# Where the attention's log-count tiles are masked, and where the out-degrees are summed

## The reference, cut to what matters

```python
aw = einsum(q[src], k[dest]); m = segment_max(aw, src); e = exp(aw - m[src])      # 8 heads, 20000 edges
alpha = e / segment_sum(e, src)[src];  out = segment_sum(alpha * v[dest], src)
deg_out = clip(segment_sum(ones, src), 1)      # third layer; deg_in likewise from dst
```

## Time and profile before

| | |
|---|---|
| median of 3 runs | 852.57 us (851.87 to 854.69) |
| profiled execution | 853.61 us, span of its instructions 851.6 us |
| PE busy | 803.9 us (94%) |
| DVE busy | 571.5 us (67%) |
| ACT busy | 395.4 us (46%) |
| mean granted TensorE clock | 0.983 |
| DMA | 126.65 MB |

### The profile page before, as it was taken

One profiled execution on the slowest core, in us unless ns is written; L12 is line 12 of the kernel. 1 busy time (PEld: TensorE's weight loads), 2 busy tenths in 40 slices (PEclk: granted clock), 3 DMA queues, 4 the chain that ended last, 5 costly groups with the idle time before them and its releaser, 6 DMA issues.

```text
span 851.6 us, 16427 instructions
## 1 busy us (share of the span) xinstructions
PE 803.9 (94%) x5245; PEld 550.0 (65%) x5245; DVE 571.5 (67%) x1869; ACT 395.4 (46%) x710; POOL 213.1 (25%) x382
## 2 busy tenths in 40 slices
PE   5998998999999999999999989999987999987996
PEld 2456555447777777877778766777755445666673
DVE  6479989546777988888778446555557835975121
ACT  1334444546667667676666533333331223533331
POOL 4200000000021122022022332222228822574443
PEclk9999999999999999999999989999999999997998
DMA  9909977688100443332483636555515470085550
GB/s 251 347 19 226 230 215 212 144 285 239 34 27 30 124 134 97 107 84 62 158 299 107 201 109 178 175 163 167 165 53 146 114 222 25 25 277 129 186 167 19
DMA packets 89029, 126.65 MB, mean 149 GB/s; under 512 B 41071, under 2 KB 50447, under 8 KB 88686
## 3 DMA queue, kind: packets, MB, share of 16 engines
q1 hardware_dynamic: 75342, 107.45, 42.5%
q0 software_dynamic: 13600, 18.11, 7.5%
HBM read 64.89 MB, written 63.33 MB: 151 GB/s over the span
## 4 chain that ended last, share of the span: by engine, by line
PE 75%; DVE 12%; DMA 4%; POOL 3%; issue 3%; ACT 1%; SPq 1%; DVEq 0%; POOLq 0%; ACTq 0%
PE ps L805 18%; PE ps L687 11%; PE ps L698 10%; PE ps L716 10%; PE ps L936 6%; PE ps L614 5%; DVE R_B L1922 4%; PE ps L812 4%; PE ps L619 4%; DVE R_B L1921 2%; PE ps L967 2%; DMA R_A<-slots_d 1%; PE ps L758 1%; DMA slots_d<-R_B,slot 1%; PE ps L555 1%
## 5 line engine op out<-in xcount | busy, mean ns | idle before, releaser
L805 PE MATMUL ps<-R_B,R_A 128*128 x612 | 184.1, 443 | 1.7 <-ACT R_A L1476 0.6
L805 PEld LDWEIGHTS ps<-R_B,R_A 128*128 128x128 f32 x612 | 110.9, 192 | 34.3 <-issue 24.5
L1281 ACT ACTIVATE R_A<-R_A,neg_max 125x1250 f32<-125x1250 f32 x80 | 106.4, 1330 | 19.1 <-DVE neg_max L1966 19.1
L1966 DVE CUSTOM_DVE_ANT_0 R_A<-ps,R_B,neg_max 125x417 f32<-125x417 f32 (+1 forms) x160 | 96.2, 648 | 21.2 <-PE ps L687 21.2
L698 PEld LDWEIGHTS ps<-ident,R_A 125*125 125x125 f32 x800 | 93.7, 188 | 14.8 <-issue 13.2
L698 PE MATMUL ps<-ident,R_A 125*125 125x125 f32 x800 | 102.0, 277 | 0.7 <-ACT XN L1224 0.7
L687 PE MATMUL ps<-R_B 64*125 64x417 f32 (+1 forms) x480 | 101.7, 536 | 0.2
L716 PE MATMUL ps<-R_W,XN 125*64 125x125 f32 x1600 | 94.7, 272 | 1.1
L716 PEld LDWEIGHTS ps<-R_W,XN 125*64 125x64 f32 x1600 | 85.5, 136 | 15.5 <-issue 14.2
L1288 ACT ACTIVATE R_W<-ps 125x500 f32<-125x500 f32 x120 | 66.1, 586 | 48.7 <-PE ps L698 48.7
L614 PE MATMUL ps<-XT,R_W 128*128 128x500 f32 (+1 forms) x192 | 72.4, 522 | 0.7 <-ACT XT L1207 0.7
(11 more groups left out here) (280 smaller groups left out, 1169.4 us busy)
## 6 DMA issues: line engine op xcount, KB each, us to landing
slots_d<-R_B SPq DMA_DIRECT2D x9, 2322.0 KB, 10.7
R_B<-in_L_ffn_w_dram SPq DMA_DIRECT2D x28, 512.0 KB, 8.2
R_A<-slots_d SPq DMA_DIRECT2D x27, 256.0 KB
slots_d<-R_A SPq DMA_DIRECT2D x27, 256.0 KB
counts_d<-R_A SPq DMA_DIRECT2D x10, 546.9 KB
logs_d<-R_B SPq DMA_DIRECT2D x10, 546.9 KB
R_B<-counts_d SPq DMA_DIRECT2D x10, 546.9 KB
R_B<-logs_d SPq DMA_DIRECT2D x9, 546.9 KB
```

The costliest lines, as they stand in the source:

```text
L805: ins = pe.matmul(bank(b, TM, width), lhs[:, c * TM:c * TM + TM], flat[:, bass.ds(e * (n * width) + c * width, width)], start=c == 0, stop ...
L1281: act.activation(SC[u % 2][h], SC[u % 2][h], ACT.Exp, bias=neg_max[:, 2 * (u % 2) + h:2 * (u % 2) + h + 1], scale=-1.0, accum_out=den[:, 2 ...
L1966: dve.tensor_tensor_reduce(SC[u % 2][h][:, a:z], bank(2 * h + g % 2, P, z - a), logs[:, a:z], -1.0, least if t else 3.0e38, ALU.add, ALU.m ...
```

## The change

`mask_logs` keeps only its first operation, for the source tile 0; what it left in `logs_d` for the other nine tiles is now unmasked, and the store waits for ACT's logarithm and no longer for DVE. The nine tiles are masked after they are loaded, in LNB, by one operation over 1250 columns for each (`mask_tile(i)`), at the end of unit 4(i-1)+1: u = 1, 5, 9, ..., 33 for i = 1 to 9. The wait for the load moves with it. ACT waits, before it overwrites a log stage, for the small mask of block b-2. SyncE waits for all ten small masks before its first load of count rows. The out-degrees are summed at the ends of units 12, 15, 16, 19, 20, 23, 24, 27, 28 and 31 in place of 12, 14, ..., 30. SyncE's list keeps its order.

```diff
-OUT_DEGREE_AT = 12
+OUT_DEGREE_OF = {u: n for n, u in enumerate((12, 15, 16, 19, 20, 23, 24, 27, 28, 31))}
@@ SyncE
-                sp.wait_ge(S("ln_masked"), b + 1)
+                sp.wait_ge(S("ln_made"), b + 1)
                 move(logs_d[:, b * P:b * P + P].rearrange("(i p) d -> p i d", p=P), ln_stage[b % 2], logs_out[b % 2])
...
+            sp.wait_ge(S("ln_masked"), T)
             load_counts_of(range(5))
@@ ACT, counts_and_logs
                 above_zero(act, logs_out[k], (b - k) * 16)
+                above_zero(act, S("ln_masked"), b - 1)
@@ DVE
             def mask_logs(b, k):
                 dve.wait_ge(S("ln_made"), b + 1)
-                first, rest = ln_stage[k][:, 0, :], ln_stage[k][:, 1:T, :]
+                first = ln_stage[k][:, 0, :]
                 own = LN0[:, b * P:b * P + P] if isinstance(b, int) else LN0[:, bass.ds(b * P, P)]
-                dve.scalar_tensor_tensor(own, first, FAR, first, ALU.mult, ALU.min)
-                dve.scalar_tensor_tensor(rest, rest, FAR, rest, ALU.mult, ALU.min).then_inc(S("ln_masked"), 1)
+                dve.scalar_tensor_tensor(own, first, FAR, first, ALU.mult, ALU.min).then_inc(S("ln_masked"), 1)
...
                     if t == 0:
-                        if u == 0:
-                            dve.wait_ge(S("ln_masked"), T)
-                        elif j == 0:
-                            dve.wait_ge(logs_in[i % 2], 32 * (i // 2) + 32 * (i % 2))
+                        if j == 0:
+                            dve.wait_ge(S("ln_masked"), T + i)
...
+                def mask_tile(i):
+
+                    dve.wait_ge(logs_in[i % 2], 32 * (i // 2) + 32 * (i % 2))
+                    dve.scalar_tensor_tensor(LNB[i % 2], LNB[i % 2], FAR, LNB[i % 2], ALU.mult, ALU.min)\
+                       .then_inc(S("ln_masked"), 1)
...
-                    if u >= OUT_DEGREE_AT and u % 2 == 0 and u < OUT_DEGREE_AT + 2 * T:
-                        out_degree((u - OUT_DEGREE_AT) // 2)
+                    if u % PAIRS == 1 and u // PAIRS + 1 < T:
+                        mask_tile(u // PAIRS + 1)
+                    if u in OUT_DEGREE_OF:
+                        out_degree(OUT_DEGREE_OF[u])
```

## The result

| | before | after |
|---|---|---|
| median | 853.57 us (851.87 to 854.69, 4 runs) | **881.11 us** (878.15 to 886.23, 4 runs) |
| ratio | | **1.0322** (95%: 1.029 to 1.0354) |
| profiled execution | 853.61, span 851.6 | 886.23, span 884.4 |
| mean granted clock | 0.983 | 0.971 |

The changed kernel is slower by 27.5 us; forecast were 20, with a range of 862 to 880, just missed. The direction, the places and the mechanism were those of the forecast; several sizes were not.

What follows compares the result with a forecast made beforehand. Counting was taken as bound mostly by DVE, the attention by TensorE. The terms -8.5 + 3.3 + 4.4 + 3.7 + 10.8 + 6.3 gave +20.0 us, on the median of 852.6 a forecast of 872.6 us, range 862 to 880.

Steps and rivals of the forecast that it cites:

- stop of tile 9: Attention: the moved last out-degree sum delays the load to 447.5, so the score operation is 11.0 late: +10.8 us.
- counting: Counting stage: large masks removed from DVE; block-by-block sum 7.0, up to 9.9 with DVE running ahead; taken as -8.5 us.
- behind the attention: The rest of the kernel after the attention only shifts, its loads waiting for TensorE's and DVE's own progress: no loss.
- out-degree sums, in themselves: Attention: the moved sums fit DVE's idle time at the ends of units with u % 4 = 3: cost 0.
- five early masks: Attention units 5, 9, 13, 17, 21, logs already landed: TensorE loses 0.65 us at each, +3.3 us.
- stop of tile 7: Attention: logs' last traffic at 379.95, mask until 381.4, score operation 4.6 late, less 0.15 slack: +4.4 us.
- stop of tile 8: Attention: logs' last traffic at 409.8, mask ends at 411.2, score operation 3.8 late: +3.7 us.
- clock behind the three: TensorE after the three long stops: granted clock drops each time, losing 1.7, 1.7 and 2.9: +6.3 us.
- The load overtaking: Attention: tile 9's load gets in place at 440.4, its stop shrinks to 3.7: 865.5 us, chance 0.10.
- the stops without a clock drop: Attention: stops cost no clock drop, or DVE takes part of them back: +13.7, 866 us, chance 0.16.
- The fourth rival: Waits longer than they look, counting squeezing the transfers, or counting winning only 6 us: 878 us and more, chance 0.12.
- The faster outcome: Attention: the late loads come in time and counting wins: -3.3, 849 us, chance 0.04.

Runs made afterwards that it cites:

- e5: The kernel before with only the out-degree sums moved to units 12, 15, 16, ..., 31, masks in counting as before: 864.33 us, ratio 1.0117.
- e8: The changed kernel with an empty operation in place of the mask of nine tiles, behind the same wait: 870.92 us, ratio 1.0177.
- second look: The changed kernel run once more, unaltered, for a second profile: 879.07 us, ratio 1.0283 to the kernel before.
- e6: The changed kernel with the out-degree sums back in units 12, 14, ..., 30, all else as changed: 873.03 us, ratio 1.0202.
- e4: The changed kernel with each mask one unit later, right before the score operation that needs it: 866.56 us, ratio 1.0133.
- The first experiment: The changed kernel with only SyncE's list reordered, every load of logs issued as soon as its buffer is free: 852.76 us, ratio 0.9986.
- e2: The changed kernel with only tile 9's load of logs put ahead of its store and the expert loads: 863.96 us, ratio 1.0108.

## Why the prediction was right, and where it was not

The median of 881.11 us lies above the range of 862 to 880. The mechanism held, and four terms of the sum had the wrong size. First, the late loads were taken to be usable at their last traffic, and the waits ended 0.5 to 0.6 us behind it: 1.7 us over the three stops. Second, in "the load at 422.5 + 25.0 = 447.5" the last traffic came 26.8 us behind the store, not 25.0; with the first this makes the stop of tile 9 13.3 us where 10.8 were forecast. Third, counting gave 6.95 us, not 8.5. Fourth, "The rest of the kernel, behind the attention, only shifts" put at 0 what was 6.9 and 3.8 us in two profiles, and its cause is open. The ends of its own terms reached from 856 to 881; the median fell into the corner that it left out.

| step | forecast us | measured us | |
|---|---|---|---|
| counting | -8.5 | -6.95 | 1.5 too much |
| out-degree sums, in themselves | 0 | 0 beside the masks | 0.7 and 1.0 in e5 and e8 |
| five early masks | +3.3 | +3.3 | right |
| stop of tile 7 | +4.4 | +4.85 | 0.45 short |
| stop of tile 8 | +3.7 | +4.5 | 0.8 short |
| stop of tile 9 | +10.8 | +13.3 | 2.5 short |
| clock behind the three | +6.3 | +6.8 | sum right, parts not |
| end of the attention | +20.0 | +25.9 | |
| behind the attention | 0 | +6.9, second look +3.8 | open |

- **Counting.** The block-by-block sum, 7.0, was the measurement. What failed was "The eight slots let DVE run ahead while TensorE is the limit, and it spends that lead in block 7": block 7 takes 127.67 - 117.72 = 9.95 us and no less. By the starts of the blocks 1.24 us are saved in block 2 and in block 3, 0.83 in block 4, 0.52 in 5 and 6 together, 1.26 and 1.25 in 7 and 8, and 0.6 from block 9 on. The clock of 68 to 72 us stayed at 1.00 where it had been 0.57; that bought nothing to see, as block 3 is DVE's. The window after:
```profile
68.00:72.00 4.00, 3.79 (x24) 2.61 (x23) 4.00 (x19) 2.84 (x6) 0.00 (x0) 1.00 1.16 166
```
  The run without masks, at 6.5 us, is in line with it.
- **Early masks.** The starts of L749 stand 31.25 us apart between tiles at 251.84 and 283.09, where 30.56 stood (440.84 - 410.28). All five together give 3.3. The clock did not fall behind stops of 0.35 to 0.7 us (granted 1.00 from 215 to 360 us). The sums, in the same tiles, add nothing there: with the sums back (e6) these tiles are as long.
- **Tiles 7 and 8.** The stops ran 0.5 and 0.8 over. The last traffic came where it was forecast (379.95 and 409.8, moved by the -3.65 and +3.85 us won and lost up to then, give 376.3 and 413.65; it ended at 376.2 and 413.9). But the masks start 0.5 and 0.6 us behind it, where the forecast let them start at once; that makes 4.9 and 4.3. The run with the wait alone shows them 1.4 to 1.6 shorter, which is the mask's own 1.37: wait plus mask.
- **Tile 9** carried the largest error. The step was "25.0 us behind the end of the last out-degree sum", a distance copied from another moment. The time of that sum came out: 422.5, moved by -6.95 and by the 3.3, 4.85, 2.65, 4.5 and 2.6 us lost up to then, gives 433.45, and the store that follows it is issued at 433.47. But the mask started only at 460.91. Of the 2.5 us missing, 0.6 are again the time from the last traffic to the end of the wait. The rest, 1.8, is the transfers: their last traffic was at 441.1 before, 25.0 us behind the issue of the store, and now at 460.3, 26.8 us behind it. It was 25.2 with the sums back (425.91 to 451.1) and 26.2 in the second look (432.35 to 458.6). The list is the same in all, and in these four so are the bytes. The traffic before (416 to 441.2 us), after (433.4 to 461), and with only the sums moved (423.3 to 452.5):

```profile
DMA packets 4517, 7.57 MB, mean 300 GB/s; under 512 B 551, under 2 KB 2087, under 8 KB 4515
...
DMA packets 4517, 7.55 MB, mean 274 GB/s; under 512 B 552, under 2 KB 2088, under 8 KB 4516
...
DMA packets 5366, 8.41 MB, mean 288 GB/s; under 512 B 582, under 2 KB 2935, under 8 KB 5363
```
  So the changed kernel moved no more, only more slowly. With only the sums moved it is another case, 29.1 us to the end of the wait (423.34 to 452.46): three expert loads that stand behind the logs in SyncE's list were issued from 443.25 on, before the logs were there, and 0.8 MB more was moved. The run with the mask before its use (e4) has the same, 8.31 MB and 28.9 us. SyncE's list, after:

```profile
433.47 0.75 SPq L338 DMA_DIRECT2D planes_d<-R_A  x2
...
437.17 4.60 SPq L404 DMA_DIRECT2D R_B<-in_L_ffn_w_dram  x8
...
441.81 8.58 SPq L409 DMA_DIRECT2D R_B<-in_L_ffn_w_dram  x3
...
450.43 1.85 SPq L338 DMA_DIRECT2D R_B<-logs_d  x2
```
  With the sums back:
```profile
425.91 0.75 SPq L338 DMA_DIRECT2D planes_d<-R_A  x2
...
433.86 6.80 SPq L409 DMA_DIRECT2D R_B<-in_L_ffn_w_dram  x3
```
  The three issues of W1E took 8.6 us after, 6.8 with the sums back, and 5.5 before. Why the same bytes moved more slowly is open; no run varied the traffic alone.
- **The clock.** The tiles behind the three stops were too long by 2.65, 2.6 and 1.5 us once the next stop is taken off: 418.76 - 381.06 = 37.70 is 30.56 + 4.49 + 2.65. The forecast gave the longest stop the most (2.9), and it cost least: wrong in the parts and near in the sum. By windows of 2 us the clock was at 0.50 for some 5.4 us after TensorE was back at 381.06, 5.2 us after 418.76, and 3.2 us after 465.19; half of each is about the loss. With the sums back the stop of tile 9 was 3.61 us, and the tile behind it was too long by 1.45 us (488.96 - 456.00, less 31.51). The Trainium skill, "TensorE: Matmul & The Clock Gate" (What's actually happening), says that idleness halves the clock and sustained work releases it; the windows above agree with 0.50, 0.50 and, over six us in which the clock came back, 0.63.
- **Behind the attention.** I had it shift only. The profiled execution lost 6.9 us more there, the second look 3.8; the nine other experiments lie between -1.4 and +3.9 by the same reading. Single executions spread by some 5 us there, and none reaches 6.9. TensorE's waits for transfers of `slots_d` behind the attention were 2.5 us before, 7.2 in the profiled execution and 4.4 in the second look, so 4.7 of the 6.9 us stand there; whether it belongs to the change stays open.
- **The rivals.** The load overtaking and the stops without a clock drop did not happen. The fourth rival, waits longer than they look and counting at 6 to 7 us, has the sizes that came; its cause, counting squeezing the transfers, does not show in tiles 7 and 8, whose traffic ended where it was forecast. The faster outcome failed where it was said to be decided: the logs landed at 376.7, 414.5 and 460.9, and DVE had waited for them since 372.6, 410.7 and 448.3. It needed another order of SyncE's list. The first experiment changed that, and then the loads were in time, but the time was 852.76 us where this rival had 849: no gain that can be told from none (ratio 0.9964 to 1.0009).

## What to carry to other kernels

An operation moved behind a load asks for that load earlier than the one that used it. Look up in the trace when the load lands and, in the in-order list of the queue that issues it, what stands ahead and which operation releases that: here moving five sums by one unit, which cost 0.7 us in itself, cost 9.4 us, by way of a store, eleven loads and one wait. And a load is not usable at its last traffic: add what the trace shows between that and the end of a wait, here 0.5 to 0.6 us. On an engine that is 84% busy beside one at 99.6%, cost lies in the place: the same nine operations cost 0.65 us each at one unit's end, 0.8 in front of their use, and nothing where the trace shows 2.2 us of idle time.

## What the runs showed of the hardware

A wait for a load ended 0.4 to 0.7 us after the last traffic of that load, in eleven waits of four profiles (the changed kernel twice, e2 and e6). The same list of transfers on one queue, a store and eleven loads of 512 KB ahead of the logs, with the same 7.55 to 7.57 MB moved, took 25.0, 25.2, 26.2 and 26.8 us from the store's issue to the last traffic of the logs, in the kernel before, in e6 and in the changed kernel's two profiles. In e4 and e5 the logs were waited for 28.9 and 29.1 us from the store's issue, and loads issued behind them on the same queue moved bytes in that time. And the clock's loss was not in order of the stop: 4.85 and 4.49 us of idleness were followed by a loss of 2.65 and 2.6 us, 13.29 us by one of 1.5, and 3.61 us in e6 by one of 1.45.
